# Pre-LN scan-and-experts layer on 8 cores: LN1's inverse roots on GpSimd, and its statistics, norms and turns moved

## The chip, the cores and the metric

The kernel runs on the 8 cores of one Trainium2 chip. Each core does the same program on its own batch row, and the cores exchange nothing. The time is the device time of the slowest core, in microseconds (us). Within a core, PE (TensorE) does the matmuls into PSUM, DVE (VectorE), ACT (ScalarE) and POOL (GpSimd) do the elementwise work, and SP issues most of the DMAs. Every engine works through its own instruction list strictly in order and waits on semaphores.

## What is computed

Input x is (8, 2048, 1024) in f32; a core holds one (2048, 1024) row. The reference, cut to what matters:

```python
def _layernorm(x, eps=1e-5): return (x - mean(x)) / sqrt(var(x) + eps)

# attention-like part
h = rmsnorm(layernorm(x), gamma)           # == layernorm without eps, times gamma
q, kv, a = split(h @ w_qkva.T, 3)          # 1024 -> 3 * 1024
y[t] = sigmoid(a[t]) * y[t-1] + kv[t]      # scan over the 2048 tokens
x = x + q * y
# experts
z = layernorm(x)
gate = softmax(z @ Wg + bg)                # 8 experts
x = x + sum_e gate[e] * (relu(z @ W1[e] + b1[e]) @ W2[e] + b2[e])
```

## The kernel before

**Chunks and phases.** The 2048 tokens are cut into four chunks of 512 (c = 0 to 3). A chunk goes through phase A (`phase_a`, LN1 output times w_qkva, scan, product) and phase F (`phase_f`, the experts). The program order is A0, A1, F0, A2, F1, A3, F2, F3, with hardly a break on PE.

**Phase A** has eight groups j, one for each 128 output features. A group has three projections of eight 128x512 matmuls each: a (bank `ba`), kv (`bk`) and q (`bq`). ACT takes the sigmoid of a (L598), DVE scans (L604), copies the carry (L609) and multiplies with q (L613). In chunk 0 PE also turns the residual x into feature order (L619) in a fourth bank and DVE adds it (L623); in the others POOL adds it in SBUF (L627). ACT then makes the bf16 copy and the square of the sum (`cs_step`, L371 and L372). The banks come from a ring of five PSUM banks (`ring_take`), and each bank's next user waits for the engine that read it last.

**Phase F** takes the experts four at a time ("quads"). `open_quad` takes four of the five ring banks and opens each with a 32-row matmul (L653); each expert adds eight matmuls (L660) and is drained by DVE into `h1g` (L663). Then two quads of output tiles follow (L653, L678), each drained by L681.

**LN1 of a chunk** is done ahead, in the phase before it. The pieces:

- statistics: `ln1_bn` (two BN_STATS and one BN_AGGR for each 128-token tile, into `mv`);
- inverse root r1 and nb1 = -mean*r1. In chunks 0 and 1 by ACT's Sqrt and DVE's reciprocal (`quick_sd`, `quick_sqrt`, `quick_r`), in chunks 2 and 3 by three Newton steps on DVE (`newton`, `ln1_small`);
- norm: `ln1_norm`, ACT writes `xn` (L280), one instruction of 128x1024 for each tile;
- turn to feature order: in chunk 1 by PE transposes, four steps kp = 0 to 3 of eight 128x128 (`ln1_turn`, L292), each evicted by two instructions (L298); in chunks 2 and 3 by DMA transposes on SP (L309) and DVE's gamma (L316).

**What sets the order.** The side work is hung on keys by hand. `(j, 0)`, `(j, 1)` and `(j, 2)` in phase A are the places after projection a, after the scan's instructions, and after the q product of group j; `("h", e)` and `("y", d)` in phase F are those after expert e and output tile d. What a hook emits lands on each engine at that point of its list, so an instruction of a hook that waits holds back all that its engine has behind it.

The places of chunk 1's LN1 before, in the code:

```python
for lo, j in ((0, 4), (2, 5)):
    add(hk, (j, 2), ...)      # statistics of tiles lo, lo+1 and quick_sd
    add(hk, (j + 1, 0), ...)  # quick_sqrt, quick_r
    add(hk, (j + 1, 1), ...)  # norms
for kp, p in enumerate([(6, 2), (6, 2), (7, 0), (7, 1)]):
    add(hk, p, lambda kp=kp: ln1_turn(1, kp))
```

`w1_sums` (eight matmuls and three DVE instructions, L562 to L569, twice) folds the LN2 bias into W1's sums; it runs in A1.

Of the kernel before, what the change touches and what calls it, by code (L numbers as in the profile page):

```python
# [875 lines left out]
```

How the kernel before makes its waits and increments, by code:

```python
        def run(eng):  # L52
            for s, v in waits:
                eng.wait_ge(s, v)
            ins = fn(eng)
            if tick:
                ins.then_inc(sem, 1)
# [8 lines left out]
        def run(eng):  # L66
            for s, v in waits:
                eng.wait_ge(s, v)
            fn(eng).then_inc(sem, 16)
# [6 lines left out]
        def run(eng):  # L76
            for s, v in waits:
                eng.wait_ge(s, v)
```

## Time and profile before

| | |
|---|---|
| time before, median of 3 runs | 339.03 us (338.90 to 339.09) |
| the profiled execution's own time | 338.64 us |
| its span (core 5, the slowest) | 337.1 us; the cores lie at 335.5 to 337.1 us |
| PE busy | 319.5 us, 95% of the span |
| DVE, ACT, POOL busy | 186.6, 102.8 and 47.7 us |
| mean granted TensorE clock, core 5 | 0.99 |

PE is the bound through almost all of the span, so what the table does not show is what counts: the few places where PE stands still or runs at the lower clock. The profile's matmuls are pipelined and their ends modelled; its POOL spans are rough.

### The profile page before, as it was taken

The numbers are of one execution on the slowest core, as the hardware profiler recorded it, in microseconds if no ns is written. First come the engines' busy times: TensorE is split into PE (matmuls) and PEld (weight loads), VectorE is DVE, ScalarE is ACT, GpSimd is POOL, SyncE is SP. The second block draws the span as 40 slices with busy tenths as digits, with TensorE's granted clock in tenths as the row PEclk, the third lists the DMA queues.
The fourth block names the chain that finished last, engine by engine and source line by source line (L and its number), as shares of the span: only waits on it lengthen the run. The fifth ranks groups of instructions, "written<-read, shape, count | busy, mean of one in ns | idle before, by whom it ended". The sixth has DMA issues, their size and how long they took to land.

```text
span 337.1 us, 4880 instructions; the slowest of 8 cores (335.5 to 337.1 us)
## 1 busy us (share of the span) xinstructions
PE 319.5 (95%) x1601; PEld 144.4 (43%) x1601; DVE 186.6 (55%) x429; ACT 102.8 (30%) x158; POOL 47.7 (14%) x64
## 2 busy tenths in 40 slices
PE   7679999499999999899999999899999999999996
PEld 2235454254444444344444444344444444444442
DVE  0835357714578469636568549536577446633433
ACT  2471315774325310411335420501425330200000
POOL 3780000011131310000312120000221220000000
PEclk9999999879999999999999999999999999999999
DMA  6999999999970300079770210099300300063023
GB/s 100 229 161 171 214 232 185 231 172 186 172 239 0 125 3 0 2 170 305 163 237 1 59 68 1 2 234 299 92 0 1 123 4 0 24 224 130 2 111 138
DMA packets 18952, 40.52 MB, mean 120 GB/s; under 512 B 10128, under 2 KB 10416, under 8 KB 17904
## 3 DMA queue, kind: packets, MB, share of 16 engines
q1 hardware_dynamic: 15632, 25.47, 25.0%
q0 software_dynamic: 3296, 14.75, 23.8%
q8 instruction: 13, 0.21, 0.3%
q14 instruction: 11, 0.09, 0.1%
HBM read 40.25 MB, written 8.42 MB: 144 GB/s over the span
## 4 chain that ended last, share of the span: by engine, by line
PE 85%; DVE 6%; issue 3%; ACT 2%; DMA 2%; DVEq 0%; SPq 0%; ACTq 0%
PE ps L591 47%; PE ps L660 16%; PE ps L678 16%; DVE bst L264 3%; DMA xtok<-xt 2%; PE ps L653 2%; PE ps L384 1%; ACT xn L280 1%; PE ps L562 1%; ACT L441 1%; PE ps L292 1%; PE ps L619 1%; PE ps L410 1%; PE ps L398 1%; DVE sc L613 0%
## 5 line engine op out<-in xcount | busy, mean ns | idle before, releaser
L591 PE MATMUL ps<-pb,wq 128*128 128x512 bf16 x768 | 172.2, 382 | 1.4 <-DMA wq<-wqd 0.8
L591 PEld LDWEIGHTS ps<-pb,wq 128*128 128x128 bf16 x768 | 74.7, 98 | 90.2 <-issue 7.2
L660 PE MATMUL ps<-pb,w 128*128 128x512 bf16 x256 | 57.0, 379 | 0.0
L678 PE MATMUL ps<-h1g,w 128*128 128x512 bf16 x256 | 56.8, 379 | 0.0
L627 POOL TENSOR_TENSOR xb<-xb,sc 128x512 f32<-128x512 f32 x24 | 30.4, 1266 | 176.3 <-DVE sc L613 136.7
L604 DVE TENSOR_TENSOR_SCAN sc<-asig,carry,ps 128x512 f32<-128x512 f32 x24 | 30.7, 1279 | 36.6 <-ACT sqr L372 19.9
L598 ACT ACTIVATE asig<-ps 128x512 f32<-128x512 f32 x32 | 19.1, 597 | 102.0 <-PE ps L591 89.4
L681 DVE TENSOR_TENSOR xb<-ps,xb 128x512 f32<-128x512 f32 x32 | 22.1, 691 | 31.8 <-PE ps L678 31.7
L678 PEld LDWEIGHTS ps<-h1g,w 128*128 128x128 bf16 x256 | 24.4, 98 | 29.9 <-issue 1.8
L660 PEld LDWEIGHTS ps<-pb,w 128*128 128x128 bf16 x256 | 24.3, 98 | 30.1 <-issue 2.2
L663 DVE SCALAR_TENSOR_TENSOR h1g<-ps,grep 128x512 bf16<-128x512 f32 x32 | 21.9, 685 | 16.1 <-PE ps L660 15.8
L613 DVE TENSOR_TENSOR sc<-ps,sc 128x512 f32<-128x512 f32 x32 | 22.1, 692 | 7.6 <-PE ps L591 6.8
L280 ACT ACTIVATE xn<-xtok,nb,r 128x1024 bf16<-128x1024 f32 x12 | 14.2, 1233 | 39.3 <-DVE nb L274 36.4
L371 ACT ACTIVATE pb<-xb 128x512 bf16<-128x512 f32 x32 | 19.9, 623 | 4.0 <-POOL xb L627 4.0
L604 DVE TENSOR_TENSOR_SCAN sc<-asig,ps 128x512 f32<-128x512 f32 x8 | 9.8, 1221 | 19.3 <-PE ps L591 19.3
L372 ACT ACTIVATE sqr<-xb 128x512 bf16<-128x512 f32 x32 | 19.8, 619 | 0.0
L264 DVE BATCH_NORM_STATS2 bst<-xtok 128x6 f32<-128x512 f32 x24 | 15.6, 684 | 7.2 <-DMA xtok<-xt 7.2
L431 PE MATMUL ps<-grep 128*128 128x512 bf16 x41 | 11.9, 449 | 1.9 <-DVE grep L189 1.9
L345 ACT ACT_TABLE_LOAD x4 | 5.1, 1283 | 17.4 <-DVE s L343 17.4
L431 PEld LDWEIGHTS ps<-grep 128*128 128x128 bf16 x41 | 4.4, 111 | 7.7 <-issue 5.2
L292 PE MATMUL ps<-identb,xn 128*128 128x128 bf16 x32 | 3.3, 258 | 4.3 <-ACT xn L280 4.3
L532 POOL DMA_DIRECT2D w<-w2d x2 | 1.1, 552 | 43.8 <-ACT pb L371 43.8
(101 smaller groups left out, 173.3 us busy)
## 6 DMA issues: line engine op xcount, KB each, us to landing
xtok<-xt SPq DMA_DIRECT2D x12, 512.0 KB, 11.6
outd<-xb SPq DMA_DIRECT2D x12, 512.0 KB, 3.8
wq<-wqd POOLq DMA_DIRECT2D x7, 768.0 KB, 25.9
grep<-gscr SPq DMA_DIRECT2D x4, 1024.0 KB, 5.6
xb<-xd SPq DMA_DIRECT2D x8, 512.0 KB, 5.7
w<-xt POOLq DMA_DIRECT2D x4, 512.0 KB, 32.2
xb<-xd POOLq DMA_DIRECT2D x4, 512.0 KB, 50.8
w<-w1d POOLq DMA_DIRECT2D x2, 1024.0 KB, 55.7
```

What stands on the lines that cost most here:

```text
L264: t = DVE.do(lambda e, h=h: e.bn_stats(bst[:, i, h, :], tok_of[c][:, i, h * TC:(h + 1) * TC]), xt_t[c][i])
L371: t1 = ACT.do(lambda e: e.activation(xbf_of[c][:, k, :], src, AF.Copy), C[c]["x2"][k], prior)
L372: t2 = ACT.do(lambda e: e.activation(sqr[b][:], src, AF.Square), C[c]["x2"][k], sq_free[b])
L591: mm[i] = PE.do(lambda e, k=k: e.matmul(ps[banks[i]][:], wq[:, j, i, k, :], hbc[:, k, :], start=(k == 0), stop=(k == KC - 1)), h[k] if j = ...
L598: sg = ACT.do(lambda e: e.activation(asig[asl][:], ps[ba][:], AF.Sigmoid), mm[0], as_free[asl])
L604: sn = DVE.do(lambda e: e.tensor_tensor_scan(sc[s][:], asig[asl][:], ps[bk][:], init, ALU.mult, ALU.add), sg, mm[1], sc_free[s], st["carry ...
L613: at = DVE.do(lambda e: e.tensor_tensor(sc[s][:], ps[bq][:], sc[s][:], ALU.mult), mm[2], cy)
L627: x2 = POOL.do(lambda e: e.tensor_tensor(xc[:, j, :], xc[:, j, :], sc[s][:], ALU.add), at, x_t[c][j])
L660: t = PE.do(lambda e, k=k: e.matmul(ps[b][:], w1[:, e_, k, :], xbf_of[c][:, k, :], start=False, stop=(k == KC - 1)), C[c]["xbf"][k] if e_ ...
L663: mt = DVE.do(lambda e: e.scalar_tensor_tensor(h1g[:, e_, :], ps[b][:], 0.0, grep[:, e_, :], ALU.max, ALU.mult), t, C[c]["gi"], st["h1g"])
L678: t = PE.do(lambda e, e_=e_: e.matmul(ps[b][:], w2[:, d, e_, :], h1g[:, e_, :], start=False, stop=(e_ == E - 1)), C[c]["h1g"][e_], w2_t[d ...
L681: o = DVE.do(lambda e: e.tensor_tensor(xc[:, d, :], ps[b][:], xc[:, d, :], ALU.add), t, C[c]["cs"][d][1], C[c]["cs"][d][2])
```

## The change

For chunks 1 to 3 the inverse root is seeded on DVE (`ln1_seed`: maximum, shift, subtract) and refined by three Newton steps on GpSimd, 12 instructions and then 2 for nb1, each of which waits for the one ahead of it. ACT's square roots and DVE's reciprocals go for chunk 1, the Newton steps on DVE go for chunks 2 and 3. BN_AGGR and the seed of a later pair of tiles now wait for the POOL steps of the pair before (`st["mv"]`, `st["va"]`). Chunk 1's statistics, norms and turns get other keys, and one turn step is evicted by DVE. The statistics of chunks 2 and 3 move from phase F into the phase A before it, the seed and the POOL steps go to `("h", 0)`, the norms to `("h", 4)` and `("h", 5)`, the DMA transposes to `("h", 7)` and gamma one output tile earlier. `w1_sums` moves within A1 from (6, 2) and (7, 2) to (5, 0) and (6, 0).

```diff
             if 1 in halves:
-                C[c]["bn"][i] = DVE.do(lambda e: e.bn_aggr(mv[:, i, :], ...), t)
+                C[c]["bn"][i] = DVE.do(lambda e: e.bn_aggr(mv[:, i, :], ...), t,
+                                         st["mv"])
-        def ln1_small(c):
-            t = DVE.do(lambda e: e.tensor_scalar_max(va[:], mv[:, :, 1], 9.765625e-33), C[c]["bn"][NT - 1])
-            for t in newton(va, t, r1[:], C[c - 1]["xn"][NT - 1]):
-                yield
-            C[c]["r1"] = DVE.do(lambda e: e.scalar_tensor_tensor(nb1[:], mv[:, :, 0], -1.0, r1[:],
-                                                                 ALU.mult, ALU.mult), t)
-            yield
+        def ln1_seed(c, lo, hi):
+            sl = slice(lo, hi)
+            t = DVE.do(lambda e: e.tensor_scalar_max(va[:, sl], mv[:, sl, 1], 9.765625e-33), C[c]["bn"][hi - 1],
+                       st["va"])
+            t = DVE.do(lambda e: e.tensor_scalar(ry[:, sl].bitcast(I32), va[:, sl].bitcast(I32), 1, None,
+                                                 ALU.arith_shift_right), t)
+            C[c]["seed"] = DVE.do(lambda e: e.tensor_scalar(ry[:, sl].bitcast(I32), ry[:, sl].bitcast(I32), -1.0,
+                                                            1597463007.0, ALU.mult, ALU.add), t)
+        def ln1_small(c, lo, hi):
+            sl = slice(lo, hi)
+            t = C[c]["seed"]
+            for it in range(3):
+                t = POOL.do(lambda e: e.tensor_tensor(ya[:, sl], ry[:, sl], ry[:, sl], ALU.mult), t)
+                t = POOL.do(lambda e: e.tensor_tensor(ya[:, sl], ya[:, sl], va[:, sl], ALU.mult), t)
+                t = POOL.do(lambda e: e.tensor_scalar(ya[:, sl], ya[:, sl], -0.5, 1.5, ALU.mult, ALU.add), t)
+                out = r1 if it == 2 else ry
+                t = POOL.do(lambda e, out=out: e.tensor_tensor(out[:, sl], ry[:, sl], ya[:, sl], ALU.mult), t,
+                            C[c - 1]["xn"][NT - 1] if it == 2 else None)
+            st["va"] = t
+            t = POOL.do(lambda e: e.tensor_tensor(nb1[:, sl], mv[:, sl, 0], r1[:, sl], ALU.mult), t)
+            C[c]["r1"] = POOL.do(lambda e: e.tensor_scalar(nb1[:, sl], nb1[:, sl], -1.0, None, ALU.mult), t)
+            st["mv"] = C[c]["r1"]
...
-        def ln1_turn(c, kp):
+        def ln1_turn(c, kp, dve=False):
...
+                if dve:
+                    ev = DVE.do(lambda e, k=k, src=src: e.tensor_scalar_mul(dst[:, k, :], src, gam[:, k:k + 1]), t, gam_t)
...
-        for lo, j in ((0, 4), (2, 5)):
-            add(hk, (j, 2), lambda lo=lo: (ln1_bn(1, lo), ln1_bn(1, lo + 1), quick.update({lo: quick_sd(1, lo, lo + 2)})))
-            add(hk, (j + 1, 0), lambda lo=lo: (quick_sqrt(1, lo, lo + 2, quick[lo]), quick_r(1, lo, lo + 2)))
-            add(hk, (j + 1, 1), lambda lo=lo: (ln1_norm(1, lo), ln1_norm(1, lo + 1)))
+        for lo, p in ((0, ((4, 0), (4, 1), (5, 1))), (2, ((5, 0), (5, 1), (6, 1)))):
+            add(hk, p[0], lambda lo=lo: (ln1_bn(1, lo), ln1_bn(1, lo + 1)))
+            add(hk, p[1], lambda lo=lo: (ln1_seed(1, lo, lo + 2), ln1_small(1, lo, lo + 2)))
+            add(hk, p[2], lambda lo=lo: (ln1_norm(1, lo), ln1_norm(1, lo + 1)))
...
-        for kp, p in enumerate([(6, 2), (6, 2), (7, 0), (7, 1)]):
-            add(hk, p, lambda kp=kp: ln1_turn(1, kp))
+        for kp, p in enumerate([(7, 0), (7, 1), (7, 2), (7, 2)]):
+            add(hk, p, lambda kp=kp: ln1_turn(1, kp, dve=(kp == 2)))
...
+        def bn_hooks(hooks, c):
+            for n, p in enumerate([(5, 2), (6, 2), (7, 1), (7, 2)]):
+                add(hooks, p, lambda n=n: ln1_bn(c, n))
...
-        add(hk, (6, 2), lambda: w1_sums(0))
-        add(hk, (7, 2), lambda: w1_sums(1))
+        add(hk, (5, 0), lambda: w1_sums(0))
+        add(hk, (6, 0), lambda: w1_sums(1))
+        bn_hooks(hk, 2)
...
+            add(hooks, ("h", 0), lambda: ln1_seed(c, 0, NT))
+            add(hooks, ("h", 0), lambda: ln1_small(c, 0, NT))
             for n in range(NT):
-                add(hooks, ("h", n), lambda n=n: ln1_bn(c, n))
-            slices(hooks, lambda: ln1_small(c), [("h", 4), ("h", 5), ("h", 6)])
-            for n in range(NT):
-                add(hooks, ("h", 7) if n < 2 else ("y", 0), lambda n=n: ln1_norm(c, n))
-            for n in range(NT):
-                add(hooks, ("y", 1), lambda n=n: ln1_turn_dma(c, n))
+                add(hooks, ("h", 4 + n // 2), lambda n=n: ln1_norm(c, n))
+                add(hooks, ("h", 7), lambda n=n: ln1_turn_dma(c, n))
             for k in range(KC):
-                add(hooks, ("y", 5 + k // 4), lambda k=k: ln1_gamma(c, k))
+                add(hooks, ("y", 4 + k // 4), lambda k=k: ln1_gamma(c, k))
```

**DVE in chunk 0, groups 4 and 5.** DVE's list from the residual add of group 4 (`xb0<-ps4,sc0`) to the scan of group 5 (`sc1<-asig1,ps1`), before. `d_xtp2` and its like are the loads of chunk 1's tiles into w2's space.

```order
L623 TENSOR_TENSOR xb0<-ps4,sc0 128x512 [waits s_pe,s_dve]
L264 BN_STATS bst<-w2 128x6 [waits d_xtp0]
L264 BN_STATS bst<-w2 128x6
L267 BN_AGGR mv<-bst 128x2 [waits s_dve]
L264 BN_STATS bst<-w2 128x6 [waits d_xtp1]
L264 BN_STATS bst<-w2 128x6
L267 BN_AGGR mv<-bst 128x2 [waits s_dve]
L436 TENSOR_SCALAR va<-mv 128x2 [waits s_dve]
L444 RECIPROCAL r1<-sd1 128x2 [waits s_act]
L446 SCALAR_TENSOR_TENSOR nb1<-mv,r1 128x2 [waits s_dve]
L551 TENSOR_SCALAR wgs<-ps7 128x8 [waits s_pe]
L604 SCALAR_TENSOR_TENSOR sc1<-asig1,ps1 128x512 [waits s_pe]
```

The same place in the changed kernel (its line numbers are some 2 to 23 higher):

```order
L646 TENSOR_TENSOR xb0<-ps4,sc0 128x512 [waits s_pe,s_dve]
L266 BN_STATS bst<-w2 128x6 [waits d_xtp2]
L266 BN_STATS bst<-w2 128x6
L269 BN_AGGR mv<-bst 128x2 [waits s_dve,s_pool]
L266 BN_STATS bst<-w2 128x6 [waits d_xtp3]
L266 BN_STATS bst<-w2 128x6
L269 BN_AGGR mv<-bst 128x2 [waits s_dve]
L574 TENSOR_SCALAR wgs<-ps7 128x8 [waits s_pe]
L627 SCALAR_TENSOR_TENSOR sc1<-asig1,ps1 128x512 [waits s_act,s_pe]
L632 COPY carry<-sc1 128x1 [waits s_dve]
L275 TENSOR_SCALAR va<-mv 128x2
L277 TENSOR_SCALAR ry<-va 128x2 [waits s_dve]
```

Tiles 0 and 1 are now done one group earlier, the second pair stands where the first did, and its first BN_AGGR waits for POOL.

**PE in chunk 0, group 7.** PE's list from the residual turn of group 6 (`xtok`, x4) to the start of A1 (`wq`, x32), before; L292 is chunk 1's turn.

```order
L619 MATMUL ps<-ident,xtok 128x128 x4
L292 MATMUL ps<-identb,xn 128x128 x16
L591 MATMUL ps<-pb,wq 128x512 x8
L292 MATMUL ps<-identb,xn 128x128 x8
L591 MATMUL ps<-pb,wq 128x512 x8
L292 MATMUL ps<-identb,xn 128x128 x8
L591 MATMUL ps<-pb,wq 128x512 x8
L619 MATMUL ps<-ident,xtok 128x128 x4
L591 MATMUL ps<-pb,wq 128x512 x32
```

The same place in the changed kernel, where L312 is that turn:

```order
L642 MATMUL ps<-ident,xtok 128x128 x4
L614 MATMUL ps<-pb,wq 128x512 x8
L312 MATMUL ps<-identb,xn 128x128 x8
L614 MATMUL ps<-pb,wq 128x512 x8
L312 MATMUL ps<-identb,xn 128x128 x8
L614 MATMUL ps<-pb,wq 128x512 x8
L642 MATMUL ps<-ident,xtok 128x128 x4
L312 MATMUL ps<-identb,xn 128x128 x16
L614 MATMUL ps<-pb,wq 128x512 x32
```

One projection now stands ahead of the first turn, and two turn steps stand right ahead of A1.

**DVE in F0, experts 4 to 7.** DVE's list from the drain of expert 4 on, before (L663 is a drain):

```order
L663 SCALAR_TENSOR_TENSOR h1g<-ps,grep 128x512
L271 TENSOR_SCALAR va<-mv 128x4
L246 TENSOR_SCALAR rr<-va 128x4
L248 TENSOR_SCALAR rr<-rr 128x4
L251 TENSOR_TENSOR aa<-rr 128x4
L252 SCALAR_TENSOR_TENSOR bb<-aa,va 128x4
L254 SCALAR_TENSOR_TENSOR rr<-bb,rr 128x4
L663 SCALAR_TENSOR_TENSOR h1g<-ps,grep 128x512
L251 TENSOR_TENSOR aa<-rr 128x4
```

In the changed kernel the whole of A1's end and of the expert part of F0 reads on DVE:

```order
L632 COPY carry<-sc 128x1
L266 BN_STATS bst<-xtok 128x6 x2
L269 BN_AGGR mv<-bst 128x2
L636 TENSOR_TENSOR sc<-ps,sc 128x512
L266 BN_STATS bst<-xtok 128x6 x2
L269 BN_AGGR mv<-bst 128x2
L686 SCALAR_TENSOR_TENSOR h1g<-ps,grep 128x512
L275 TENSOR_SCALAR va<-mv 128x4
L277 TENSOR_SCALAR ry<-va 128x4
L279 TENSOR_SCALAR ry<-ry 128x4
L686 SCALAR_TENSOR_TENSOR h1g<-ps,grep 128x512 x7
```

Statistics stand ahead of the first drain, three seed instructions behind it, and nothing between the other seven.

## Rows read from the trace of the kernel before

**Rows 1.** PE's waits over the whole span: total us, times, longest us

```profile
PE ps L292 <- ACT xn L280: 4.3, 2, 3.5
PE ps L653 <- DVE nb L274: 1.8, 2, 1.0
```

**Rows 2.** The chain that ended last, group 7 of chunk 0: start us, us, what

```profile
74.15 0.45 PE ps L292 x8
74.60 1.73 PE ps L591 x8
76.32 0.44 PE ps L619 x4
76.76 6.91 PE ps L591 x32
```

**Rows 3.** Timeline of chunk 0, groups 3 to 7: start us, us, engine, what

```profile
44.33 0.69 DVE L623 TENSOR_TENSOR xb<-ps,sc 128x512 f32<-128x512 f32 x1
...
47.36 1.22 DVE L604 TENSOR_TENSOR_SCAN sc<-asig,ps 128x512 f32<-128x512 f32 x1 [2.33 <-PE ps L591]
...
48.68 0.15 DVE L609 COPY carry<-sc 128x1 f32<-128x1 f32 x1
...
49.16 0.69 DVE L613 TENSOR_TENSOR sc<-ps,sc 128x512 f32<-128x512 f32 x1 [0.32 <-PE ps L591]
...
49.95 0.69 DVE L623 TENSOR_TENSOR xb<-ps,sc 128x512 f32<-128x512 f32 x1
50.56 1.27 DVE L264 BATCH_NORM_STATS2 bst<-w 128x6 f32<-128x512 f32 x2
...
51.94 0.21 DVE L267 BATCH_NORM_AGGREGATE mv<-bst 128x2 f32<-128x12 f32 x1
...
53.43 0.21 DVE L267 BATCH_NORM_AGGREGATE mv<-bst 128x2 f32<-128x12 f32 x1
...
55.59 0.17 DVE L444 RECIPROCAL r<-sd 128x2 f32<-128x2 f32 x1 [1.68 <-ACT sd L441]
...
56.07 1.22 DVE L604 TENSOR_TENSOR_SCAN sc<-asig,ps 128x512 f32<-128x512 f32 x1
...
61.83 0.60 PE L619 MATMUL ps<-ident,xtok 128*128 128x128 f32 x4
...
64.61 2.37 ACT L280 ACTIVATE xn<-w,nb,r 128x1024 bf16<-128x1024 f32 x2 [0.63 <-DVE nb L446]
...
66.00 0.27 PE L292 MATMUL ps<-identb,xn 128*128 128x128 bf16 x1 [3.46 <-ACT xn L280]
...
68.47 3.51 PE L591 MATMUL ps<-pb,wq 128*128 128x512 bf16 x8
```

**Rows 4.** Windows of 2 us: busy by engine, then PEclk, DMA share, GB/s

```profile
64.00:66.00 2.00, 0.00 (x1) 0.03 (x1) 1.65 (x4) 1.39 (x2) 0.00 (x0) 0.73 1.02 221
66.00:68.00 2.00, 1.14 (x10) 0.97 (x11) 1.38 (x2) 2.00 (x4) 0.46 (x1) 0.50 0.98 178
```

**Rows 5.** DMA issues of 14.8 to 15.3 us: median us to landing

```profile
w<-xt POOLq DMA_DIRECT2D x1, 512.0 KB, 28.6
```

**Rows 6.** DMA issues of 16.3 to 17 us: median us to landing

```profile
w<-xt POOLq DMA_DIRECT2D x2, 512.0 KB, 35.4
```

**Rows 7.** POOL's timeline at the start of the kernel

```profile
1.20 0.12 POOL L177 MEMSET sele<- 128x32 bf16 x1
1.45 0.10 POOL L178 MEMSET sele<- 128x1 bf16 x1
...
14.59 0.37 POOL L514 CAST wgx<-wgf 128x128 bf16<-128x128 f32 x1
```

**Rows 8.** Groups by form: count, busy us, mean ns, idle before

```profile
L627 POOL TENSOR_TENSOR xb<-xb,sc 128x512 f32<-128x512 f32 x24 | 30.4, 1266 | 176.3 <-DVE sc L613 136.7 <-DVE hi L347 14.8 <-DVE rr L246 13.2
```

**Rows 9.** Timeline of DVE's Newton steps in F0

```profile
136.35 0.16 DVE L251 TENSOR_TENSOR aa<-rr 128x4 f32<-128x4 f32 x1
136.62 0.16 DVE L252 SCALAR_TENSOR_TENSOR bb<-aa,va 128x4 f32<-128x4 f32 x1
```

More of the change, by code:

```diff
@@ L152, in build_program @@
         va = sb("va", [128, NT], F32)
+        ry = sb("ry", [128, NT], F32)
+        ya = sb("ya", [128, NT], F32)
         r1 = sb("r1", [128, NT], F32)
@@ L214, in build_program @@
         xn_free = [None] * NT
-        st = {"psT": None, "rowsb": None, "tm": ms["tm"], "grep": None, "h1g": None, "carry": [None] * KC}
+        st = {"va": None, "mv": None, "psT": None, "rowsb": None, "tm": ms["tm"], "grep": None, "h1g": None, "carry": [None] * KC}
         C = [dict(x2=[None] * KC, xbf=[None] * KC, h=[None] * KC, bn=[None] * NT, xn=[None] * NT,
@@ L266, in ln1_bn @@
             if 1 in halves:
-                C[c]["bn"][i] = DVE.do(lambda e: e.bn_aggr(mv[:, i, :], bst[:, i, :, :].rearrange("p a b -> p (a b)")), t)
-        def ln1_small(c):
-            t = DVE.do(lambda e: e.tensor_scalar_max(va[:], mv[:, :, 1], 9.765625e-33), C[c]["bn"][NT - 1])
-            for t in newton(va, t, r1[:], C[c - 1]["xn"][NT - 1]):
-                yield
-            C[c]["r1"] = DVE.do(lambda e: e.scalar_tensor_tensor(nb1[:], mv[:, :, 0], -1.0, r1[:],
-                                                                 ALU.mult, ALU.mult), t)
-            yield
+                C[c]["bn"][i] = DVE.do(lambda e: e.bn_aggr(mv[:, i, :], bst[:, i, :, :].rearrange("p a b -> p (a b)")), t,
+                                         st["mv"])
[21 more added lines that the diff above has]
+            st["mv"] = C[c]["r1"]
         def ln1_norm(c, i):
@@ L297, in ln1_turn @@
             for k in (2 * kp, 2 * kp + 1):
-                ev = ACT.do(lambda e, k=k: e.activation(dst[:, k, :], pbf[:, (k % 2) * TC:(k % 2 + 1) * TC], AF.Copy,
-                                                        scale=gam[:, k:k + 1]), t, gam_t,
-                            C[c - 1].get("pe_q") if c >= 2 else None)
+                src = pbf[:, (k % 2) * TC:(k % 2 + 1) * TC]
+                if dve:
+                    ev = DVE.do(lambda e, k=k, src=src: e.tensor_scalar_mul(dst[:, k, :], src, gam[:, k:k + 1]), t, gam_t)
+                else:
+                    ev = ACT.do(lambda e, k=k, src=src: e.activation(dst[:, k, :], src, AF.Copy, scale=gam[:, k:k + 1]),
+                                t, gam_t)
                 C[c]["h"][k] = ev
@@ L436, in quick_sd @@
             t = DVE.do(lambda e: e.tensor_scalar_max(va[:, lo:hi], mv[:, lo:hi, 1], 9.765625e-33),
-                       C[c]["bn"][hi - 1], C[0]["sd"] if c else None)
+                       C[c]["bn"][hi - 1])
             return t
@@ L443, in quick_r @@
         def quick_r(c, lo, hi):
-            t = DVE.do(lambda e: e.reciprocal(r1[:, lo:hi], sd1[:, lo:hi]), C[c]["sd"],
-                       C[c - 1]["xn"][NT - 1] if c else None)
+            t = DVE.do(lambda e: e.reciprocal(r1[:, lo:hi], sd1[:, lo:hi]), C[c]["sd"])
             C[c]["r1"] = DVE.do(lambda e: e.scalar_tensor_tensor(nb1[:, lo:hi], mv[:, lo:hi, 0], -1.0, r1[:, lo:hi],
@@ L498, in build_program @@
         ACT.do(lambda e: e.activation(warm[:, 1:2], warm[:, 0:1], AF.Sigmoid))
+        st["va"] = C[0]["sd"]
         st["psT"], psR_free[0], psR_free[1], ring_free[4] = [C[0]["h"][k] for k in (2, 3, 6, 7)]
@@ L745, in build_program @@
         gate = {}
-        quick = {}
-        for lo, j in ((0, 4), (2, 5)):
-            add(hk, (j, 2), lambda lo=lo: (ln1_bn(1, lo), ln1_bn(1, lo + 1), quick.update({lo: quick_sd(1, lo, lo + 2)})))
-            add(hk, (j + 1, 0), lambda lo=lo: (quick_sqrt(1, lo, lo + 2, quick[lo]), quick_r(1, lo, lo + 2)))
-            add(hk, (j + 1, 1), lambda lo=lo: (ln1_norm(1, lo), ln1_norm(1, lo + 1)))
+        for lo, p in ((0, ((4, 0), (4, 1), (5, 1))), (2, ((5, 0), (5, 1), (6, 1)))):
+            add(hk, p[0], lambda lo=lo: (ln1_bn(1, lo), ln1_bn(1, lo + 1)))
+            add(hk, p[1], lambda lo=lo: (ln1_seed(1, lo, lo + 2), ln1_small(1, lo, lo + 2)))
+            add(hk, p[2], lambda lo=lo: (ln1_norm(1, lo), ln1_norm(1, lo + 1)))
         add(hk, (5, 0), lambda: gate.update(t=gate_sums()))
-        for kp, p in enumerate([(6, 2), (6, 2), (7, 0), (7, 1)]):
-            add(hk, p, lambda kp=kp: ln1_turn(1, kp))
+        for kp, p in enumerate([(7, 0), (7, 1), (7, 2), (7, 2)]):
+            add(hk, p, lambda kp=kp: ln1_turn(1, kp, dve=(kp == 2)))
         phase_a(0, hk)
@@ L787, in build_program @@
         stat_hooks(hk, 2)
+        bn_hooks(hk, 3)
         phase_a(2, hk)
```

## Prediction

> **What bounds the kernel now.** I read the busy table first: PE is busy for 95% of the span, so a change of this kind pays only where PE waits or runs slowly. The list of PE's waits shows, behind the start of the kernel, which the change leaves alone, two that belong to LN1 [rows 1]: 4.3 us at L292, the turn of chunk 1, and 1.8 us at L653, the opening of an output quad in F0 and F1. The chain of waits then gives the price of the first. The last turn of the residual in group 6 starts at 61.83 [rows 3] and takes 0.44 like its twin in group 7 [rows 2], so PE is free at 62.27. From there to A1's start at 76.76 [rows 2] it does three projections of 1.73, four turn steps of about 0.45 and a residual turn of 0.44: 7.4 us of work in 14.5 us. **7.1 us are lost there**, more than the 4.3 of waiting, because PE comes out of the wait at the lower clock: the granted clock falls in the window from 64 to 66 us and is 0.50 (1.2 of 2.4 GHz) in the next [rows 4], after PE has stood since 62.5, and eight matmuls that take 1.73 at full clock [rows 2] take 3.51 at 68.47 [rows 3].
>
> The timeline shows where the wait comes from [rows 3]. The statistics of tiles 0 and 1 start at 50.56; DVE stands 1.68 us at the reciprocal for ACT's square root (with a table load in it), so the scan of group 5 starts only at 56.07, the second pair does the same again, and the second pair of norms starts at 64.61 and ends at 66.98, when PE has been ready for 4.7 us.
>
> **The change, part by part.**
>
> *Chunk 1, first pair.* The residual add of group 3 starts at 44.33. Before, such an add at 49.95 was followed by statistics that ended at 53.43 + 0.21 = 53.64, 3.69 later [rows 3]; so these end at 48.0. Their data are there: tile 0 was issued near 14.8 and took 28.6, about 43.4 [rows 5]. The scan of group 4, at 47.36 before, starts at 48.05 and its carry at 49.37. Three seed instructions at the 0.27 spacing of dependent small ones [rows 9] end at about 50.25, and POOL starts at 50.35. DVE goes on with product and residual add until about 51.7 (0.69 each), then BN_STATS of tile 2 (issued near 16.4, landed near 51.8 [rows 6]) and then stands in BN_AGGR until POOL has finished all 14 steps.
>
> *The unknown: one POOL step, s.* No row shows a POOL instruction on two elements with inputs. From below, the 128x1 memset takes 0.10, and it started 0.13 after the end (1.32) of the memset that it waits for: 0.23 a step [rows 7]. From above, the 128x128 cast takes 0.37, with the wait 0.50. The large addition at 1.27 for 512 elements is further off [rows 8]. I take 0.20 and 0.13, **s = 0.33**, nearer the memset since the width is the memset's, and keep 0.23 and 0.50 for the range.
>
> *The chain to the first turn.* POOL's first 14 steps end at P = 50.35 + 14 s (55.0). Then on DVE: 0.1 of wait, from BN_AGGR to the end of the second one 1.70 (51.94 to 53.64 [rows 3]), the gate sums and the scan of group 5 at about P + 1.95, carry at P + 3.3, seeds to P + 4.1. POOL again 14 s from P + 4.2; ACT's two norms 2.37 with 0.1 ahead and 0.15 to PE behind. The second xn reaches PE at 50.35 + 28 s + 6.8 = **57.15 + 28 s**, 66.4 at 0.33. PE does one projection ahead of the turn and is ready at 62.27 + 1.73 = 64.0. **PE waits 2.4 us** where it waited 4.3, but in a place with 1.73 of work put in front. A DVE wait takes the place of the square root's: behind the BN_AGGR stand tile 3's statistics and the scan, product and residual add of group 5. At P + 1.95 = 57.0 that scan is 0.9 later than before, and PE first needs its bank at 60.1 and the residual's bank at 62.3, when they end at 58.2 and 60.7. It costs PE nothing as long as P is under about 56.6.
>
> *The end of group 7.* Kp 3's turn needs the bank of q's product, which DVE reads: product end is about 1.0 after the projection, while PE's work up to there is 0.9, with the semaphore 0.25 lost. Kp 2's eviction by DVE stands behind product and residual add and is late by about 0.2 for A1's fifth and sixth matmul. I charge 0.5 together. If the clock falls again, eight matmuls and more cost 1.8 (3.5 against 1.73). Before, the lower clock came after a wait of 3.5 with little work around; 2.4 us behind a full projection is shorter, and I take no fall.
>
> Loss after: 2.4 + 0.5 = 2.9 instead of 7.1, a gain of **4.2**.
>
> *F0 and F1.* The opening of the output quad waited 1.0 and 0.8 because DVE drained expert 6 behind the Newton steps. These are gone from DVE, which has nothing between the last seven drains; gain **1.8**. POOL has the whole expert part for 14 steps (4.6 us), and ACT is idle there. What is new: statistics of 1.6 at (7, 1) and (7, 2) push group 7's product and the first drain. If the last projection of A1 ends at time 0, the product runs from 1.6 to 2.3, the next statistics to 3.9, the first drain to 4.7, seeds to 5.5, drains 1 and 2 to 6.9; the second quad opens at 0.33 + 7.0 = 7.3. It is hidden by 0.4. The DMA transposes now stand ahead of the first output store on SP, but POOL is done at about 10.2 by this count, ACT's four norms follow at 1.2 each while the experts run to 15, and the transposes go out behind each of them, ahead of the first store. `w1_sums` moves inside A1 with its 3.5 us of PE work; its DVE part, 1.9, delays a scan whose bank is wanted two projections later. The table loads that vanish on ACT were off the path apart from the one in the wait above.
>
> *Sum.* 338.64 - 4.2 - 1.8 = 332.6 against the profiled execution, whose span is 337.1 with 1.5 around it; the median of the runs is 0.4 higher, so **333.0**.
>
> **A rule against this change.** POOL's addition takes 1266 ns for 512 elements [rows 8] where DVE's residual addition of the same size takes 0.69 us [rows 3]: 1.8 times. The Trainium skill, page "GPSIMD Engine Reference", section "Engine selection", says of elementwise work to use VectorE and not GPSIMD, which is about twice as slow with two inputs; at this size the trace agrees, and no row shows it for small ones. Held against the sum, it would be rival 2, 338.1 us instead of 333.0.
>
> **The rivals.**
>
> 1. *The clock falls anyway.* Same wait of about 2.4, plus 1.8: 334.8. For it: the fall on core 5 came within about 2.5 us of standing [rows 4]. Against it: the old stand was longer. 20%.
> 2. *POOL's small step is twice DVE's.* DVE's takes 0.16 [rows 9], so s = 0.32 + 0.13 = 0.45, the xn comes at 69.75, PE waits 5.7, surely loses 1.8 to the clock behind it, and 0.5 at the end: 8.0 instead of 7.1, less 1.8 in F0 and F1: 338.1. For it speaks the ratio of the large additions, against it that the memset takes only 0.10. 11%.
> 3. *Slower: the POOL chain in series.* At s = 0.50 the xn comes at 71.15, PE waits 7.15, loses 1.8 to the clock and 0.5: 9.45 against 7.1, less 1.8 in F: 0.55 more, 339.6. It decides from s = 0.49 on, where wait, clock and end together reach 8.9. 7%.
> 4. *The drains are late.* If DVE is 1 us later at the quad that opens behind the first, 0.6 of PE's wait comes back in F0 and F1 each: 334.2. The margin of 0.4 speaks for it, DVE's even pace against. 7%.
>
> The forecast itself, s from 0.23 to 0.38 at full clock, 55%: its own range is 330.6 (s = 0.23: no wait, loss 0.5, gain 6.6 + 1.8) to 334.4.
>
> **How the numbers follow.** The likeliest case gives 333.0. The range from 330.8 to 337.2 takes in the first and fourth rival and most of the second's way, and leaves 11 + 7% above and very little below. A measurement of this kernel tells about 0.2% from no change, 0.7 us: rival 3 and a little of 2 lie beyond on the slow side, most of 2 just inside the faster side. Faster 0.88, same 0.05, slower 0.07.
>
> **What would show it.** Right: POOL's small steps spaced about 0.33, PE's one wait at chunk 1's turn of 2 to 3 us starting near 64.0, PEclk 1.00 from 62 to 76, A1 starting near 72.5, no PE wait at L676 behind the experts, DVE waiting in L269 for POOL by about 2 us near 53. Wrong: a step spacing over 0.4, any granted clock of 0.50 around 66, PE waiting for the group 5 residual's bank at 62.3, or a new wait in A1 or at the second expert quad.

## The result and the profile after

| | changed kernel |
|---|---|
| time, median | 334.5 us, against 339.1 us before |
| ratio to before | 0.9866, 95% interval 0.9842 to 0.9891 |
| a second measurement, beside experiments 8 and 9 | 334.8 us, 0.9869 (0.9854 to 0.9884) |
| span, slowest core | 332.4 us (core 0); cores at 330.7 to 332.4 us |

One of the four runs behind the median lay at 390.5 us with one die at a granted clock of 0.82; it is not in the ratio. The change made the kernel faster by **4.6 us**; 6.0 had been forecast.

The page's busy table and clock line of the changed kernel, to be read against the busy times in the table of before:

```profile
PE 315.9 (95%) x1570; PEld 144.0 (43%) x1601; DVE 185.1 (56%) x411; ACT 96.1 (29%) x150; POOL 59.2 (18%) x120
...
PEclk9999999979999999999999999999999999999999
```

POOL has 11.5 us more, ACT 6.7 less (5.5 for four table loads and the two square roots, the rest for the turn step that DVE now evicts), DVE hardly less. The engines' sums tell little; PE's waits tell more. The list of PE's waits, total us, times, longest us:

```profile
PE ps L483 <- ACT sd L464: 3.8, 3, 2.0
PE ps L312 <- ACT xn L300: 3.2, 2, 2.2
```

The first is the start of the kernel, as before. The turn of chunk 1 still waits 3.2 us against 4.3 [rows 1], and the 1.8 us at the output quads [rows 1] are gone. Where the 3.2 come from is in the timeline of chunk 0 (core 0: start us, us, engine, what, and the idle time ahead of it):

```profile
47.56 1.22 DVE L627 TENSOR_TENSOR_SCAN sc<-asig,ps 128x512 f32<-128x512 f32 x1
...
49.50 0.17 DVE L279 TENSOR_SCALAR ry<-ry 128x2 int32<-128x2 int32 x1
...
49.82 0.19 POOL L287 TENSOR_TENSOR ya<-ry 128x2 f32<-128x2 f32 x1 [26.40 <-DVE ry L279]
50.15 0.20 POOL L288 TENSOR_TENSOR ya<-ya,va 128x2 f32<-128x2 f32 x1
...
54.70 0.23 POOL L295 TENSOR_SCALAR nb<-nb 128x2 f32<-128x2 f32 x1 [0.16 <-POOL nb L294]
...
55.03 0.21 DVE L269 BATCH_NORM_AGGREGATE mv<-bst 128x2 f32<-128x12 f32 x1 [2.74 <-POOL nb L295]
...
56.79 1.22 DVE L627 TENSOR_TENSOR_SCAN sc<-asig,ps 128x512 f32<-128x512 f32 x1
...
59.05 0.20 POOL L287 TENSOR_TENSOR ya<-ry 128x2 f32<-128x2 f32 x1 [4.12 <-DVE ry L279]
...
63.53 0.23 POOL L295 TENSOR_SCALAR nb<-nb 128x2 f32<-128x2 f32 x1 [0.16 <-POOL nb L294]
63.85 2.37 ACT L300 ACTIVATE xn<-w,nb,r 128x1024 bf16<-128x1024 f32 x2 [4.94 <-POOL nb L295]
65.23 0.22 PE L312 MATMUL ps<-identb,xn 128*128 128x128 bf16 x1 [2.24 <-ACT xn L300]
...
66.36 0.44 PE L312 MATMUL ps<-identb,xn 128*128 128x128 bf16 x5 [0.91 <-ACT xn L300]
66.86 2.92 PE L614 MATMUL ps<-pb,wq 128*128 128x512 bf16 x7
```

In the last lines PE turns each part of xn as ACT finishes it; its next projection, at 66.86, runs at the lower clock. Two POOL chains of 14 steps lie one behind the other, from 49.82 to 54.93 and from 59.05 to 63.76; DVE stands in BN_AGGR for the first (2.74 us), and its seeds for the second end 4.0 us after that chain. A step is 0.37 us in the first chain (5.11 / 14) and 0.34 in the second (4.71 / 14).

A figure used below is **d**: from the start of group 6's residual turn to the start of A1 on PE, by the weight loads of each core's trace. Its work is 7.4 + 0.44 = 7.8 us. Before, d is 13.7 to 15.3 us; in the changed kernel it is 13.5 on cores 0, 3 and 6 and 10.9 to 11.8 on the other five. The clock fell on the first three alone. Not all of the difference is its price, since four of the other five also waited less at the turn (1.8 to 2.5 us against 3.1 to 3.2); core 4 waited 3.2 us like core 0, kept its clock and has 11.8, so the fall costs **1.7 us**. The windows of 66 to 68 and 68 to 70 us on core 0 (busy by engine, then PEclk, DMA share, GB/s):

```profile
66.00:68.00 2.00, 1.58 (x9) 0.89 (x11) 0.00 (x0) 2.00 (x5) 1.17 (x2) 0.78 1.04 174
68.00:70.00 2.00, 2.00 (x10) 0.90 (x9) 0.12 (x1) 0.89 (x2) 0.00 (x0) 0.50 0.97 158
```

and on core 4:

```profile
66.00:68.00 2.00, 1.14 (x9) 0.70 (x10) 0.00 (x0) 2.00 (x4) 0.72 (x2) 1.00 0.86 152
68.00:70.00 2.00, 2.00 (x17) 1.17 (x16) 0.86 (x1) 1.82 (x4) 0.45 (x1) 1.00 1.05 180
```

F0, from its first quad to A2, lasts 29.05 us against 30.26, F1 29.05 against 30.07: 2.2 us. A1 is 0.1 longer, A2 0.3 longer, A3 0.2 shorter. On the slowest cores the bill is d 14.87 to 13.51, F 2.2, A1 to A3 -0.2, and 1.3 by which core 0 of the one run had its first groups sooner than core 5 of the other: 4.7 of span.

The 1.4 of d and the 1.3 are better taken together. A core whose PE comes to the turn sooner has longer to wait there (cores 0, 3 and 6, the earliest, wait 3.1 to 3.2 us), and over the eight cores group 6's residual turn starts at 60.0 to 62.3 in both kernels. What counts is when A1 starts, by the first weight load of its first 32 matmuls, before (core 5) and in the changed kernel (core 0):

```profile
76.49 1.50 PEld L591 LDWEIGHTS ps<-pb,wq 128*128 128x128 bf16 x8
...
73.78 0.58 PEld L614 LDWEIGHTS ps<-pb,wq 128*128 128x128 bf16 x4
```

Chunk 0 gives 2.7 us by this, on the slowest cores and in the mean of the eight alike (75.7 to 73.0), and F0, F1 and A1 to A3 give 2.0.

### The profile page after: what moved, and what is told of

Read it like the earlier page. It is cut to its first block, busy times and chain, and to the rows that moved or that the text cites. A ratio compares the mean times of both kernels' runs of the same rounds, so it can differ in the third digit from the quotient of the medians.

```text
span 332.4 us, 4912 instructions; the slowest of 8 cores (330.7 to 332.4 us)
## 1 busy us (share of the span) xinstructions
PE 315.9 (95%) x1570; PEld 144.0 (43%) x1601; DVE 185.1 (56%) x411; ACT 96.1 (29%) x150; POOL 59.2 (18%) x120
## 4 chain that ended last, share of the span: by engine, by line
PE 81%; DVE 7%; issue 5%; DMA 2%; ACT 2%; POOL 2%; DVEq 0%; POOLq 0%; SPq 0%; ACTq 0%
PE ps L614 42%; PE ps L683 17%; PE ps L701 16%; DVE bst L266 2%; DMA xtok<-xt 2%; PE ps L676 2%; PE ps L407 1%; DVE sc L627 1%; ACT xn L300 1%; PE ps L585 1%; PE ps L312 1%; PE ps L433 1%; PE ps L421 1%; PE ps L642 1%; DVE bb L254 0%
## 5 line engine op out<-in xcount | busy, mean ns | idle before, releaser
L614 PE MATMUL ps<-pb,wq 128*128 128x512 bf16 x750 | 169.8, 381 | 2.1 <-issue 0.6
L650 POOL TENSOR_TENSOR xb<-xb,sc 128x512 f32<-128x512 f32 x24 | 30.5, 1269 | 159.2 <-DVE sc L636 119.6
L627 DVE TENSOR_TENSOR_SCAN sc<-asig,ps 128x512 f32<-128x512 f32 x8 | 9.8, 1220 | 16.8 <-PE ps L614 14.5
L454 PE MATMUL ps<-grep 128*128 128x512 bf16 x40 | 11.1, 434 | 2.0 <-DVE grep L191 1.9
L287 POOL TENSOR_TENSOR ya<-ry 128x2 f32<-128x2 f32 (+1 forms) x12 | 2.4, 197 | 34.7 <-DVE ry L279 33.6
L300 ACT ACTIVATE xn<-w,nb,r 128x1024 bf16<-128x1024 f32 x4 | 4.7, 1232 | 8.5 <-POOL nb L295 8.5
```

The source lines that it names most:

```text
L300: C[c]["xn"][i] = ACT.do(lambda e: e.activation(xn[:, i, :], tok_of[c][:, i, :], AF.Identity, bias=nb1[:, i:i + 1], scale=r1[:, i:i + 1]), ...
L614: mm[i] = PE.do(lambda e, k=k: e.matmul(ps[banks[i]][:], wq[:, j, i, k, :], hbc[:, k, :], start=(k == 0), stop=(k == KC - 1)), h[k] if j = ...
L627: sn = DVE.do(lambda e: e.tensor_tensor_scan(sc[s][:], asig[asl][:], ps[bk][:], init, ALU.mult, ALU.add), sg, mm[1], sc_free[s], st["carry ...
L650: x2 = POOL.do(lambda e: e.tensor_tensor(xc[:, j, :], xc[:, j, :], sc[s][:], ALU.add), at, x_t[c][j])
```

## The experiments

Each was timed in five rounds beside the kernel before; the ratio is to that. The kernel before had medians of 339.1 to 339.6 us beside the different experiments, so a difference of medians between experiments that were not timed side by side is good to some 0.3 us.

**1. The turns alone.** The kernel before, with only this:

```diff
-        for kp, p in enumerate([(6, 2), (6, 2), (7, 0), (7, 1)]):
-            add(hk, p, lambda kp=kp: ln1_turn(1, kp))
+        for kp, p in enumerate([(7, 0), (7, 1), (7, 2), (7, 2)]):
+            add(hk, p, lambda kp=kp: ln1_turn(1, kp, dve=(kp == 2)))
```

> The kernel before with only the four turn steps of chunk 1 at their new places (and one eviction on DVE); square roots on ACT, statistics and Newton steps as before. If the gain in chunk 0 comes from the projection that now stands ahead of the first turn, this has it all: the second xn is as late as before, PE stands 3.1 us instead of 4.3 and loses about 2 less beside it, A1 starts 12 to 13.5 us after group 6's residual turn instead of 14.3 to 15.3, and the time is 336.5 to 337.5 us, 2.2 above the changed kernel. The rival: it is the roots on GpSimd that bring the xn earlier; then this one stays at 338.5 to 339 us.

Measured: 337.9 us, 0.9956 (0.9944 to 0.9968), between the two, 1.5 us faster than before. On the slowest core, core 1, PE waits the 3.1 us that were expected, on the others 2.6 to 3.7 (the trace names DVE's product of group 6 as the releaser, which holds the turn's bank; it ends at 66.76, the xn at 67.01, so both were late together; the row is that of core 1):

```profile
PE ps L292 <- DVE sc L616: 3.1, 1, 3.1
```

d is 11.3 to 14.9 us, and six of eight cores fall to the lower clock (all eight do before). So one projection put in front of the turn is worth 1.5 us without any GpSimd; that the gain in chunk 0 comes from the turns' place alone was too much, and 337.9 is above the 336.5 to 337.5 expected. Part of the gap lies behind chunk 0: F1 lasts 30.4 us and A3 44.5 to 44.6, 0.35 and 0.2 longer than before. No run looks for the cause; in experiment 10 it is gone.

**2. Square roots kept on ACT, everything two places earlier.** On top of experiment 1:

```diff
         for lo, j in ((0, 4), (2, 5)):
-            add(hk, (j, 2), ...)      # statistics and quick_sd
-            add(hk, (j + 1, 0), ...)  # quick_sqrt, quick_r
-            add(hk, (j + 1, 1), ...)  # norms
+            add(hk, (j, 0), ...)
+            add(hk, (j, 1), ...)
+            add(hk, (j, 2), ...)
```

> The one before it with chunk 1's statistics, roots and norms two hook places earlier (statistics at (4,0) and (5,0), square root on ACT at (4,1) and (5,1), norms at (4,2) and (5,2)). The theory that the POOL chain is what makes the changed kernel's xn late says that here the xn is ready near 60.6, ahead of PE's 64.0, with at most 0.7 us of waiting for group 6's banks behind the later sigmoid (two table loads are back): no lower clock, 332.5 to 334 us without any gain in F0 and F1. The rival, that ACT's square root with its table loads costs DVE and PE as much as GpSimd's 14 steps: 336 us or more.

Measured: 333.8 us, 0.9839 (0.9826 to 0.9852): faster than the changed kernel, with nothing gained in F0 (30.3 us) and F1 0.35 longer than before (30.4), as in experiment 1. The timeline (core 1) has the second pair's norms 6.4 us ahead of the changed kernel's, and PE's turn waits 0.19 us, for the bank of group 6's product. On the other cores this wait is 0 to 1.3 us, more than the 0.7 that was expected at most:

```profile
55.06 1.28 ACT L444 ACT_TABLE_LOAD   x1
...
57.50 2.36 ACT L280 ACTIVATE xn<-w,nb,r 128x1024 bf16<-128x1024 f32 x2
...
64.37 0.69 PE L292 MATMUL ps<-identb,xn 128*128 128x128 bf16 x8 [0.19 <-DVE sc L616]
```

d is 8.3 to 9.8 us and no core's clock falls. From DVE's maximum at 54.81 to the norm at 57.50 the square root with its table load takes 2.7 us; seed and POOL chain take 5.7 for the same (58.19 to 63.85). In chunk 0 the roots on GpSimd are the slower way.

**3. The second pair does not wait for the first pair's POOL steps.** The two pairs use other columns of `mv` and `va`.

```diff
-                C[c]["bn"][i] = DVE.do(..., t, st["mv"])
+                C[c]["bn"][i] = DVE.do(..., t, st["mv"] if c > 1 else None)
...
-            t = DVE.do(... C[c]["bn"][hi - 1], st["va"])
+            t = DVE.do(... C[c]["bn"][hi - 1], st["va"] if c > 1 or lo == 0 else None)
```

> The changed kernel without the wait of the second pair's BN_AGGR and seed for GpSimd's steps of the first pair (they touch other columns of mv and va, so nothing is raced). The theory of the series, 57.15 + 28 s, says that DVE's 2.7 us of standing go, the second pair's seeds are there as GpSimd ends the first 14 steps, the xn reaches PE about 3 us earlier and PE stands under 0.5 us at the turn, with no fall of the clock: 329.5 to 331.5 us. The rival, that GpSimd alone is the bound and the wait costs nothing: 334.4 us again.

Measured: 330.6 us, 0.9746 (0.9732 to 0.9759). The timeline (core 0) shows BN_AGGR without a wait for POOL; what comes late here is the data of tile 2 itself:

```profile
52.56 1.29 DVE L266 BATCH_NORM_STATS2 bst<-w 128x6 f32<-128x512 f32 x2 [1.11 <-DMA w<-xt]
...
53.95 0.21 DVE L269 BATCH_NORM_AGGREGATE mv<-bst 128x2 f32<-128x12 f32 x1
...
62.77 2.37 ACT L300 ACTIVATE xn<-w,nb,r 128x1024 bf16<-128x1024 f32 x2 [2.25 <-POOL nb L295]
```

PE's list of waits has no entry for the turn on this core, at most 0.7 us on others, d is 8.3 on five cores and 9.2 on three, and no clock falls. For chunk 1 the wait guarded nothing, and leaving it out is worth 3.9 us, nearly as much as the whole change. Part of what it cost is not the 2.7 us in its row but what followed: the lower clock.

**4. Chunks 2 and 3 alone.** Chunk 1's hooks are those of before, the rest is the changed kernel.

> The part for chunks 2 and 3 alone: chunk 1's statistics, square roots, norms and turns are those of before, all else is that of the changed kernel. Its phases F0 and F1 should be 1.2 and 1.0 us shorter as there, A1 and A2 0.1 and 0.3 longer, so 336.8 to 337.2 us. The rival, that the gain of F0 and F1 is given back at the start of A2 and A3 by later gammas or evictions: 338 us or more.

Measured: 337.3 us, 0.9938 (0.9924 to 0.9951), 2.1 us faster; F0 and F1 last 29.05 us each, and all cores fall to the lower clock in chunk 0 as before. Nothing that counts is given back behind F0 and F1: A2 is 0.3 longer, A3 0.2 shorter. The median is 0.1 above the range that was expected.

**5. Two Newton steps for chunk 1.**

```diff
-            for it in range(3):
+            for it in range(3) if c > 1 else (1, 2):
```

> The changed kernel with two Newton steps instead of three for chunk 1 (its inverse root is a little less exact); chunks 2 and 3 keep three. Eight of the 28 GpSimd steps in series go. If each counts with 0.35 us on the way to PE's turn, as 57.15 + 28 s has it, the second xn comes 2.8 us earlier, PE's 3.1 us of waiting go to about 0.3 and the clock does not fall on any core: 330 to 331.5 us. The rival, that the wait at the turn comes from ACT's place in the order (norms behind the sigmoid of group 6) and not from GpSimd: within 0.5 us of 334.4.

Measured: 330.3 us, 0.9739 (0.9725 to 0.9752). Eight steps less, 2.8 us of POOL time, bring 4.1 us; PE's waits at the turn are 0 to 0.6 us by core and no clock falls. The POOL chain was the last to come, as the formula of the prediction says. That its end is worth more than its own 2.8 us fits the clock, whose fall experiment 6 prices at 1.2 to 1.6.

**6. Unused matmuls in the wait.**

```diff
+        def junk(n):
+            for _ in range(n):
+                PE.do(lambda e: e.matmul(psT[:], wq[:, 0, 0, 0, :], pb[0][:, 0, :], start=True, stop=True),
+                      st["psT"], C[0]["h"][0], tick=False)
...
+        add(hk, (7, 0), lambda: junk(8))
         for kp, p in enumerate([(7, 0), (7, 1), (7, 2), (7, 2)]):
```

> The changed kernel with eight matmuls whose result nobody uses (1.73 us at full clock) ahead of chunk 1's first turn, inside the wait there. The wait of 3.1 us falls to about 1.4 and the xn is no earlier. If the stand is what lets the clock fall on cores 0, 3 and 6 of the changed kernel (A1 13.5 us after group 6's residual turn, 10.9 to 11.8 on the others), then no core falls here, all show 10.9 to 12, and the time is 332 to 333 us. The rival, that the clock has nothing to do with it and these cores only had later data: no change or, by work added on the path, 334.4 to 336 us.

Measured: 333.2 us, 0.9820 (0.9807 to 0.9834), 1.2 to 1.6 us faster than the changed kernel with more work in it. The windows of core 3, where PE still stands for more than half of 64 to 66 us:

```profile
64.00:66.00 2.00, 0.84 (x6) 0.31 (x4) 0.00 (x0) 2.00 (x2) 0.00 (x0) 1.00 0.99 182
66.00:68.00 2.00, 1.68 (x12) 0.99 (x13) 0.00 (x0) 2.00 (x5) 1.18 (x2) 1.00 1.12 182
```

The granted clock is 1.00 there and on all eight cores from 62 to 76 us, and d is 10.4 to 11.8; PE's waits at the turn are 0.2 to 1.5 us. The stand, not late data, is what lets the clock fall. The earlier xn, which this one does not have, is worth the 2.6 to 2.9 us that remain to experiments 3 and 5.

**7. Newton steps of chunks 2 and 3 on DVE, at experts 0 to 2.**

```diff
-            add(hooks, ("h", 0), lambda: ln1_seed(c, 0, NT))
-            add(hooks, ("h", 0), lambda: ln1_small(c, 0, NT))
+            slices(hooks, lambda: ln1_dve(c), [("h", 0), ("h", 1), ("h", 2)])
```

`ln1_dve` is the `ln1_small` of before.

> The changed kernel with the Newton steps of chunks 2 and 3 back on DVE, but at experts 0 to 2 of phase F, behind the statistics that stay in phase A; chunk 1 stays on GpSimd. If the 2.2 us of F0 and F1 come from what stands between the last drains (experts 4 to 6) and not from the engine, DVE has caught up long before the output quad and the time is 334.4 again, at most 0.4 more for the quad behind the first. The rival, that DVE has no room for them beside the drains: F0 and F1 give back 1 us or more, 335.4 to 336.6 us.

Measured: 337.7 us, 0.9945 (0.9931 to 0.9959); F0 and F1 last 30.3 and 30.5 us. The theory failed and the rival held, for this place, though its 335.4 to 336.6 us were too low: F0 and F1 give back 2.7 us, all that they had gained and more. DVE starts the phase late, behind the statistics that now stand in A1, and the quad behind expert 3 waits for its banks (timeline of core 5):

```profile
129.65 0.69 DVE L696 SCALAR_TENSOR_TENSOR h1g<-ps,grep 128x512 bf16<-128x512 f32 x1
...
130.49 0.40 PE L686 MATMUL ps<-gro,w1b 32*128 32x512 bf16 x4 [1.20 <-DVE nb L303]
```

**8. The same on DVE, at experts 3 to 5.** As experiment 7, with the norms behind expert 6:

```diff
+            slices(hooks, lambda: ln1_dve(c), [("h", 3), ("h", 4), ("h", 5)])
...
-                add(hooks, ("h", 4 + n // 2), lambda n=n: ln1_norm(c, n))
+                add(hooks, ("h", 6), lambda n=n: ln1_norm(c, n))
```

> The changed kernel with the Newton steps of chunks 2 and 3 on DVE behind the drains of experts 3, 4 and 5 and the norms behind expert 6. With them at experts 0 to 2 the wait only moved, to the quad that opens behind expert 3, and cost 1.2 and 1.4 us. Here that quad has its drains in time, and DVE can be up to 1.0 us late at expert 6 before the output quad waits; two slices of 1.6 us against 1.05 us free between drains make it some 1.2 us late at expert 5 and 0.5 at expert 6. If the place decides, F0 and F1 last 29.1 us as in the changed kernel, and the time is that of the changed kernel run beside it within 0.4 us. The rival, that DVE has no room anywhere in the expert part and GpSimd is what frees it: F0 and F1 at 30 us or more, 1.5 to 3 us slower than the changed kernel.

Measured: 334.5 us, 0.9861 (0.9848 to 0.9875), the changed kernel beside it 334.8. F0 and F1 last 29.05 us, to the hundredth those with GpSimd. The timeline (core 4) shows DVE idle again two drains before the output quad:

```profile
133.57 0.69 DVE L696 SCALAR_TENSOR_TENSOR h1g<-ps,grep 128x512 bf16<-128x512 f32 x1
134.18 0.15 DVE L303 SCALAR_TENSOR_TENSOR nb<-mv,r 128x4 f32<-128x4 f32 x1
134.99 0.69 DVE L696 SCALAR_TENSOR_TENSOR h1g<-ps,grep 128x512 bf16<-128x512 f32 x1 [0.66 <-PE ps L693]
136.71 0.69 DVE L696 SCALAR_TENSOR_TENSOR h1g<-ps,grep 128x512 bf16<-128x512 f32 x1 [1.03 <-PE ps L693]
```

With the statistics out of the expert part the Newton steps fit between drains on DVE. No run moves the statistics alone, or starts the Newton steps one expert earlier with the statistics left in place, so how much is due to each stays open.

**9. The changed kernel with the turns back at their old places.**

> The changed kernel with chunk 1's turn steps back at (6,2), (6,2), (7,0) and (7,1), all evicted by ACT. PE is ready for the first turn 1.73 us sooner and the xn comes when it did: it stands 4.8 us instead of 3.1 and surely falls to the lower clock. If the order of projection and turn is worth its 1.73 us and a part of the clock, this is 1.5 to 2.5 us slower than the changed kernel run beside it, 336 to 337 us, and close to the run with the part for chunks 2 and 3 alone (337.3). The rival, that the earlier statistics bring most of the gain in chunk 0: within 0.7 us of the changed kernel.

Measured: 336.6 us, 0.9926 (0.9914 to 0.9938), 1.8 us slower than the changed kernel beside it (334.8). d is 11.6 to 15.1, PE waits 2.4 to 5.0 us at the turn, and seven of eight cores fall. Against experiment 4 (337.3, 0.9938), which differs from it in chunk 1's statistics, roots and norms alone, it is 0.7 us faster by the medians and 0.4 by the ratios, whose intervals overlap. So the turns' place is worth 1.5 to 1.8 us; the earlier statistics with GpSimd under the old turns next to nothing.

**10. Early square roots with the changed chunks 2 and 3.** Experiments 2 and 4 together.

> Chunk 1 as in the run with the early square roots on ACT (no GpSimd), chunks 2 and 3 as in the changed kernel. If the two parts are independent their gains add: 333.8 less 2.1 is 331.7 us, 2.7 under the changed kernel, with square roots where it has GpSimd. The rival, that a fixed part of the time (the arrival of the weights of groups 6 and 7) takes what the earlier start gives: 332.5 to 333.8 us.

Measured: 330.8 us, 0.9747 (0.9734 to 0.9761). The gains add, and by the medians there are 0.9 us more than their sum. The phases of the slowest cores show them, from A1's start to F3's first quad: experiment 2 is 0.8 longer there than before (F1 and A3), experiment 4 is 2.2 shorter, this one 2.3. The lengthening of F1 and A3 does not come with the changed chunks 2 and 3, and A2 lasts 44.2 us as before, not 44.4 as in experiment 4.

**11. The work moved, without GpSimd.** Experiments 2 and 8 together; no root is computed on GpSimd. Its places are nearly those of the change: chunk 1's norms stand at (4, 2) and (5, 2) instead of (5, 1) and (6, 1), the Newton steps of chunks 2 and 3 at experts 3 to 5 instead of 0, and their norms behind expert 6.

> All of the change's places and none of its GpSimd: chunk 1 with square roots on ACT and everything two hook places earlier, chunks 2 and 3 with their Newton steps on DVE behind experts 3 to 5. If the places make the whole gain, this equals the run with early square roots and GpSimd for chunks 2 and 3, 330.8 us, within 0.5. The rival, that the Newton steps on DVE cost something once A1 starts earlier: 331.5 to 333 us.

Measured: 331.2 us, 0.9769 (0.9751 to 0.9788), d 8.4 to 9.8, F0 and F1 29.05. PE's waits at the turn are 0 to 1.3 us by core; on core 3, the slowest:

```profile
PE ps L322 <- DVE sc L647: 0.4, 1, 0.4
```

A kernel that moves the work and leaves the engines as they were is 3.3 us faster than the changed one. It is not faster than the changed kernel without its BN_AGGR wait (330.6, ratio 0.9746, experiment 3): by medians GpSimd is 0.6 us ahead there, by ratios 0.8, and the intervals overlap. So the engine brings under 1 us, if anything, and what costs is the wait that came with it. **The changed kernel itself** was run once more beside experiments 8 and 9:

> The changed kernel itself once more, on the chip of the other runs of this set: 334.4 us, and by its trace the spread over the cores of which some fall to the lower clock and some do not.

Measured: 334.8 us, 0.9869 (0.9854 to 0.9884). This time five cores fell, with d from 10.2 to 14.5; on core 2 the clock was at 0.50 for three windows.

The runs by what the clock did in 62 to 76 us of the profiled execution (a core "fell" where its mean granted clock there is under 1.00):

| kernel | us | cores that fell | d, us |
|---|---|---|---|
| before | 339.1 | 8 | 13.7 to 15.3 |
| chunks 2 and 3 alone (4) | 337.3 | 8 | 14.5 to 16.0 |
| turns back (9) | 336.6 | 7 | 11.6 to 15.1 |
| turns alone (1) | 337.9 | 6 | 11.3 to 14.9 |
| Newton on DVE, experts 0 to 2 (7) | 337.7 | 4 | 10.2 to 14.7 |
| Newton on DVE, experts 3 to 5 (8) | 334.5 | 6 | 10.9 to 13.5 |
| changed | 334.5, 334.8 | 3, 5 | 10.2 to 14.5 |
| unused matmuls (6) | 333.2 | 0 | 10.4 to 11.8 |
| square roots early (2, 10) | 333.8, 330.8 | 0 | 8.3 to 9.8 |
| no wait for POOL (3) | 330.6 | 0 | 8.3 to 9.2 |
| two steps (5) | 330.3 | 0 | 8.5 to 9.1 |
| no GpSimd (11) | 331.2 | 0 | 8.4 to 9.8 |

## Why the prediction was right, and where it was not

The direction and the range held (334.5 in 330.8 to 337.2), the size was 1.4 us too large. Step by step:

- **First pair and the wait in BN_AGGR.** Right. The scan of group 4 starts late behind the statistics, POOL starts 2.26 us after that scan (2.30 by the prediction), DVE stands 2.74 us in BN_AGGR, and the scan of group 5 comes 1.86 us behind POOL's end (1.95).
- **One POOL step, s.** Taken as 0.33, measured 0.37 and 0.34. 28 steps are 9.8 us instead of 9.2. On core 0 the second xn reached PE at 66.36 all the same, where 66.4 was forecast, because POOL started at 49.82 and not at 50.35; that is luck. PE waits 1.8 to 3.2 us by core, 3.2 on the slowest, instead of 2.4, for core 0's PE had done group 6 over a microsecond sooner than 62.27. The duration of one step was 0.20, as chosen; the wait between two was 0.14 and not 0.13, and the first chain has one gap of 0.49. Rival 3, the slower kernel, would begin at s = 0.48 and not at 0.49 by its own numbers.
- **"I take no fall."** This is the step that failed. The clock fell on three cores of eight and, in the other measurement, on five, and the slowest core sets the time. The price in the rival was right: 1.8 us charged, 1.7 measured between core 0 and core 4, which waited equally long (d 13.51 and 11.84; in the other measurement 13.5 and 11.8 at 3.1 us of waiting). With the xn on time, A1 starts at 73.78 instead of 72.5, and this is nearly all that the forecast was off by. Filling the stand (experiment 6) brings the time to 333.2, where 333.0 had been forecast. The rival that the clock falls anyway was given 20% and 334.8 us; it is the one that came about.
- **The end of group 7.** 0.5 was charged; where the xn is early (experiment 3), d is 8.29 and the work 7.83, so 0.46. Right.
- **F0 and F1.** 1.8 by the rows of the waits, measured 2.2, of which the longer A1 and A2 take back 0.2 net with A3; where the other 0.4 stood before, no row read here shows. The second quad was hidden, as worked out; experiment 7, where it was not, shows what that is worth.
- **The rivals on POOL's duration.** The small step does not scale like the large addition: 0.20 us against DVE's 0.16 [rows 9], 1.25 times, not 1.8. The advice of the Trainium skill (page "GPSIMD Engine Reference", section "Engine selection") against elementwise work there names about twice the time for two inputs; at this size the trace does not agree (1.25 times), and the measurement decides. What the trace has against GpSimd here is the chain: a dependent step comes every 0.34 us against 0.27 on DVE [rows 9], and 14 of them with the seed take 5.7 us where ACT's square root with its table load, a way of which that section says nothing, takes 2.7. In the time it shows only where the chain is the last to come; in experiment 3 it is almost hidden.
- **What had not been asked.** The prediction costed the BN_AGGR wait as part of the change; that it need not be there (experiment 3), and that the moved work gives at least the same gain without GpSimd (experiment 8 for chunks 2 and 3, 11 for all), no step of it had considered.

What stays open: why of two cores with the same stand of PE one keeps its clock and the other does not; and why F1 and A3 are longer in experiments 1 and 2.

## What to carry to other kernels

When work goes to another engine and to another place at once, run the places alone: here they made the whole gain (331.2 us without any root on GpSimd, 330.6 with them and the same three Newton steps, once the needless wait is gone). Look at each wait that a chain on a slow engine adds and ask whether it guards the same bytes; one token for a whole tile put two independent chains in series. And price a stand of PE twice, with and without the fall of the clock behind it: filling it with unused matmuls is worth 1.2 to 1.6 us, ending it is worth 4.
